# Mean aggregates of a graph network: gathered blocks stationary and one-hots of 64 columns moving, sums kept by feature

## The chip, the cores and the metric

One core of a Trainium2 chip runs the whole program. The metric is the device time of one execution in microseconds. TensorE (PE) multiplies; its weight loads are listed as PEld. VectorE is DVE, ScalarE is ACT, GpSimd is POOL and SyncE is SP. POOL issues the gathers, SP the plain loads and stores.

## What is computed

3125 nodes with 1024 features, 50000 edges sorted by destination. One attention layer (4 heads of 256) comes first, then two layers that take the mean over the incoming edges, all in float32. This change concerns the two mean layers:

```python
def _sage_layer(h, edge_src, edge_dst, deg_inv, W_self, W_neigh, b):
    msg = h[edge_src]
    agg = jax.ops.segment_sum(msg, edge_dst, num_segments=h.shape[0])
    mean = agg * deg_inv[:, None]
    return h @ W_self + mean @ W_neigh + b
...
h = jnp.maximum(_layernorm(x, axis=-1), 0.0)
x = x + _L0_gnn_ref(h, edge_index, ...)          # attention
h = jnp.maximum(_layernorm(x, axis=-1), 0.0)
deg_inv = 1.0 / jnp.maximum(deg, 1.0)
h1 = jax.nn.relu(_sage_layer(h, edge_src, edge_dst, deg_inv, W_self0, W_neigh0, b0))
x = x + _sage_layer(h1, edge_src, edge_dst, deg_inv, W_self1, W_neigh1, b1)
```

## The kernel before

Every float32 number is held as two float16 halves, high and low. A node's row is 2048 numbers of float16, 4096 bytes. A product of a tile with a 1024x1024 weight is 48 matmuls of 512 columns (high by high, high by low, low by high; 8 slices of the contraction, 2 halves of the columns), listed by `products`. Nodes stand in 25 tiles of 125 (TN). The program is a row of blocks, each of which begins when all engines have ended the one before: `prepare` (stage tab, tables and weight scales), the first norm and product (norm), edge scores, `weighted_sums` (gagg, the attention's sums), `gat_finish` (fin), `neighbours` (agg0, first mean, its product, relu), `sums_and_product` (agg1, second mean beside the product of the nodes' own rows), and `project` (neigh1, the product of the second mean).

A chunk is 128 edges in a row of the sorted list, cut so that it meets one tile; 415 chunks. In `prepare`, DVE places each chunk's tile and its edges (`place`, `own_row`), POOL fetches the edges' rows, PE turns the lists and DVE writes them as tables (`run_idx` the sources, `run_rel` the destinations within the tile, `run_tile` the tile). `place` runs its inner loop twice, once for the attention's order and once for that of the means.

In agg0 and agg1 POOL gathers the source rows of a chunk into one of R buffers (`got`; R is 9 and 8), 128 rows of 4 KB by an indirect DMA, as soon as PE has given the buffer back. DVE writes the one-hot mask of the chunk (`hot`, 128 edges x 128 destinations). PE holds the mask stationary and moves the gathered block, 4 matmuls of 512 columns (L2286 in agg0, L1839 in agg1). Chunks go in groups of two, or of one, 220 groups; DVE adds the sum of a group to the tile's row of `acc` (L2195, L1811), by nodes: 125 partitions x 1024 features. The group of a tile's end is followed by ACT (high half, times the inverse degree), DVE (low half, L2170), PE (16 turns of 128 columns), ACT (moves the turned halves), and 48 products in 6 pieces among the groups of the next tile (L2270), DVE's read with scale (L2178), ACT's relus (L2233), DVE's low half of the result (L2182), and SP's store. agg1 has the same ring, and the product of the nodes' own rows beside it (L1177). neigh1 takes the second mean from `acc`, splits it, turns it (L1072) and multiplies (L1090).

The order of each engine is that of the code; only semaphores connect them. On PE's queue the groups of a round and the pieces of the product stand in a fixed order.

Of the kernel before, what the change touches and what calls it, by code (L numbers as in the profile page):

```python
# [11 lines left out]
def bass_gat_sage_sage(nc, x_in, src_in, dst_in, w_gat, att_src, att_dst, gat_bias,  # L12
# [26 lines left out]
    RG = 8  # L39
    SB = 4  # L40
    CHUNKS = -(-E // CH) + NT - 1
    PAIRS = (CHUNKS - NT) // PAIR
    FOURS = (CHUNKS - 3 * NT) // 4
    GROUPS = PAIRS + NT
    EP = -(-(E + CH) // (CPP * CH))
    NCH = EP * CPP
    B = PAIR * RG
# [3 lines left out]
    paired = [min(PAIRS, CHUNKS * (r + 1) // (PAIR * NT)) for r in range(NT)]  # L51
    runs = [[tuple(range(PAIR * g, PAIR * (g + 1))) for g in range(paired[r - 1] if r > 0 else 0, paired[r])] + [(PAIR * PAIRS + r,)]
            for r in range(NT)]
# [23 lines left out]
    assert PAIR == 2 and PAIRS * PAIR + NT == CHUNKS and paired[-1] == PAIRS and NCH * CH >= E + CH and EP <= P and CHUNKS < NS  # L77
    assert 4 * FOURS + 3 * NT == CHUNKS and sum(len(cols) for cols in sets) == CHUNKS
    assert all(CHUNKS * (r + 1) // (PAIR * NT) <= PAIRS or CHUNKS * (r + 1) // NT - PAIR * PAIRS + NT - 1 - r <= r + 1 for r in range(NT))
# [101 lines left out]
    with top:  # L181
# [14 lines left out]
        run_idx = sb0("run_idx", [P, NS], i32)  # L196
        run_rel = sb0("run_rel", [P, NS])
        run_tile = sb0("run_tile", [1, NS], i32)
# [11 lines left out]
        deg_inv = sb0("deg_inv", [TN, NT])  # L210
        h1_up = sb0("h1_up", [P, 1])
        h1_down = sb0("h1_down", [P, 1])

        def tile_reg(engine, table, col):

            return nc.values_load_multi_w_load_instructions(
                table[0:1, col:col + 1], engines=[engine], min_val=0, max_val=NT - 1)[1][0]

# [5 lines left out]
        def prepare(key_r, mask_r, w16):  # L224
            with ExitStack() as ctx:
# [15 lines left out]
                start_c = sb("start_c", [P, NT - 1])  # L241
                first = sb("first", [P, NT + 1])
# [12 lines left out]
                run_size = sb("run_size", [P, 2, NT])  # L255
                run_begin = sb("run_begin", [P, 2, NT])
                run_shift = sb("run_shift", [P, 2, NT])
# [9 lines left out]
                pos_p = sb("pos_p", [SP_, 2, SB])  # L267
                own_p = sb("own_p", [SP_, 2, 2, SB])
                own_lo = sb("own_lo", [SP_, 2, SB])
                own_f = sb("own_f", [SP_, 2, SB])  # L270
                own_i = sb("own_i", [SP_, 2, SB], i32)
                own_got = sb("own_got", [SP_, 2, SB, 2 * CH], i32)
                own_rel = sb("own_rel", [SP_, 2, SB, CH])
# [1475 lines left out]
        def sums_and_product(tag, rows_in, acc, product):  # L1749

            with ExitStack() as ctx:
# [36 lines left out]
                def _(v):  # L1788
# [10 lines left out]
                    for k in range(1, R, 2):  # L1799
                        v.memset(got[:, k, :].bitcast(f32), 0.0).then_inc(blank[1], 1)  # L1800
                        if k // 2 < AHEAD:
                            make_hots(k // 2)
# [549 lines left out]
```

## Time and profile before

| what | us |
| --- | --- |
| runs of the kernel: median of 3 (lowest to highest) | 3293.75 (3290.86 to 3297.03) |
| profiled execution, first to last instruction (its span) | 3292.1 |
| of it: agg0 | 694 |
| of it: agg1 | 696 |
| of it: neigh1 | 296 |
| of it: tables (tab), about | 85 |
| PE busy / DVE busy / ACT busy / POOL busy | 2940.5 / 2208.3 / 1221.8 / 1517.3 |

The profiled execution lies 1.65 us under the median, within the spread of the runs. Stages follow one another, so a stage's share is read from a table of windows; what binds in a stage is read from the waits there, and not from the busy shares of the whole span. "Busy" of a matmul is a modelled end, so that the pace of a stream is better read from the starts of rows that follow each other.

### The profile page before, as it was taken

How to read it: one execution, taken by the hardware profiler on the slowest of the kernel's cores; microseconds unless marked ns; L12 is line 12 of the kernel's file. 1: busy time of each engine (PE TensorE's matmuls, PEld its weight loads, DVE VectorE, ACT ScalarE, POOL GpSimd, SP SyncE). 2: the span in 40 equal slices, each digit the busy share in tenths (PEclk: the TensorE clock that was granted, in tenths of full speed). 3: DMA queues.
4: the chain of work that ended last, by engine and by line, in shares of the span. 5: the costliest groups of instructions: out<-in, count | busy, mean ns of one | idle time of the engine just before them, and what ended most of it. 6: DMA issues, size and time to landing. Idle time of an engine off the chain costs nothing. (4 is left out here: it accounts for less than half of the span.)

```text
span 3292.1 us, 61715 instructions
## 1 busy us (share of the span) xinstructions
PE 2940.5 (89%) x19999; PEld 1682.0 (51%) x19999; DVE 2208.3 (67%) x3758; ACT 1221.8 (37%) x2818; POOL 1517.3 (46%) x1504
## 2 busy tenths in 40 slices
PE   5577998699999985999799999996899999998999
PEld 4344555388888873444244444443344444443444
DVE  8786878688888897888466666664455555555333
ACT  3564554598888883444122222222000000001111
POOL 2002232367777772222566666661565656552000
PEclk6688999899999998999899999998999999999999
DMA  2896996489999986776799999994999999996454
GB/s 80 273 294 212 330 311 204 157 303 363 348 361 349 352 300 202 219 219 210 293 338 350 343 353 350 363 360 165 358 340 321 340 333 339 324 355 233 137 142 126
DMA packets 271674, 934.22 MB, mean 284 GB/s; under 512 B 43263, under 2 KB 44267, under 8 KB 271375
## 3 DMA queue, kind: packets, MB, share of 16 engines
q0 software_dynamic: 206144, 709.74, 60.4%
q1 hardware_dynamic: 65230, 220.77, 21.4%
q8 instruction: 153, 2.51, 0.3%
q14 instruction: 147, 1.20, 0.1%
HBM read 838.14 MB, written 130.54 MB: 294 GB/s over the span
## 5 line engine op out<-in xcount | busy, mean ns | idle before, releaser
L1743 PE MATMUL gagg_sum_ps<-gagg_got,gagg_hot_hi 128*128 128x256 f16 x3320 | 575.8, 274 | 59.7 <-DVE sums_acc L1691 26.3
L1778 POOL DMA_INDIRECT agg_got<-h_rows,all_run_idx x415 | 412.6, 994 | 336.1 <-PE agg_sum_ps L1839 195.0
L1646 POOL DMA_INDIRECT gagg_got<-xs_rows,all_set_idx x415 | 460.3, 1109 | 169.4 <-issue 85.0
L1709 ACT ACTIVATE gagg_hot_hi<-gagg_hot,all_mem 128x128 f16<-128x128 f16 x1660 | 507.0, 387 | 81.3 <-DVE gagg_hot L1664 80.2
L2130 POOL DMA_INDIRECT agg_got<-h_rows,all_run_idx x415 | 420.8, 1014 | 251.1 <-PE agg_sum_ps L2286 139.7
L1811 DVE TENSOR_TENSOR sums_acc<-agg_sum_ps,sums_acc 125x1024 f32 x220 | 269.2, 1224 | 293.9 <-PE agg_sum_ps L1839 292.3
L1743 PE MATMUL gagg_sum_ps<-gagg_got,gagg_hot_lo 128*128 128x256 f16 x1660 | 454.8, 274 | 0.0
L1839 PE MATMUL agg_sum_ps<-agg_got,agg_hot 128*128 128x512 f16 x1660 | 400.3, 383 | 50.5 <-DMA agg_got<-h_rows,all_run_idx 40.4
L2195 DVE TENSOR_TENSOR sums_acc<-agg_sum_ps,sums_acc 125x1024 f32 x220 | 269.0, 1223 | 232.1 <-PE agg_sum_ps L2286 231.0
L2286 PE MATMUL agg_sum_ps<-agg_got,all_mem 128*128 128x512 f16 x1660 | 391.9, 382 | 22.4 <-DMA agg_got<-h_rows,all_run_idx 19.3
L1743 PEld LDWEIGHTS gagg_sum_ps<-gagg_got,gagg_hot_hi 128*128 128x128 f16 x3320 | 286.8, 97 | 111.3 <-DVE sums_acc L1691 38.0
L1839 PEld LDWEIGHTS agg_sum_ps<-agg_got,agg_hot 128*128 128x128 bf16 x1660 | 158.1, 98 | 257.5 <-DMA agg_got<-h_rows,all_run_idx 37.6
L2270 PE MATMUL agg_out_ps<-agg_w,all_mem 128*128 128x512 f16 x1200 | 283.8, 381 | 3.9 <-ACT all_mem L2225 3.9
L1177 PE MATMUL agg_out_ps<-agg_w,all_mem 128*128 128x512 f16 x1200 | 285.9, 381 | 0.0
L2286 PEld LDWEIGHTS agg_sum_ps<-agg_got,all_mem 128*128 128x128 bf16 x1660 | 160.8, 98 | 221.3 <-issue 27.3
L1669 DVE TENSOR_TENSOR gagg_hot_lo<-gagg_hot,all_mem 128x512 f16<-128x512 f16 x415 | 268.7, 687 | 3.6 <-DVE gagg_hot L1664 2.8
L1156 ACT ACTIVATE all_mem<-agg_turn_ps 128x2048 f16<-128x2048 f16 x25 | 46.9, 1877 | 598.7 <-PE agg_turn_ps L1164 598.7
L1090 PE MATMUL neigh_out_ps<-neigh_w,neigh_a_t 128*128 128x512 f16 x1176 | 259.3, 380 | 0.0
L1555 PE MATMUL edg_out_ps<-gatw_w,edg_a_t 128*128 128x512 f16 x1008 | 244.1, 387 | 16.3 <-ACT edg_rows L1363 16.3
L2270 PEld LDWEIGHTS agg_out_ps<-agg_w,all_mem 128*128 128x128 f16 x1200 | 117.8, 98 | 147.3 <-ACT all_mem L2225 4.3
L1177 PEld LDWEIGHTS agg_out_ps<-agg_w,all_mem 128*128 128x128 f16 x1200 | 118.1, 98 | 143.7 <-issue 3.6
L2217 ACT ACTIVATE all_mem<-sums_acc,all_deg_inv 125x1024 f16 x25 | 28.7, 1148 | 427.7 <-issue 392.7
(370 smaller groups left out, 4152.9 us busy)
## 6 DMA issues: line engine op xcount, KB each, us to landing
gatw_piece<-slot_rows POOLq DMA_DIRECT2D x52, 512.0 KB, 9.8
split_w<-edg_w_out SPq DMA_DIRECT2D x32, 512.0 KB, 7.7
agg_got<-h_rows,all_run_idx POOLq DMA_INDIRECT x830, 8.4
x_rows<-fin_val POOLq DMA_DIRECT2D x25, 500.0 KB
h_rows<-fin_h POOLq DMA_DIRECT2D x25, 500.0 KB
out_dram<-neigh_rows POOLq DMA_DIRECT2D x24, 500.0 KB, 3.6
norm_x_sb<-in_x_dram SPq DMA_DIRECT2D x25, 448.0 KB
fin_x_sb<-in_x_dram SPq DMA_DIRECT2D x25, 448.0 KB
```

The source lines that it names most:

```text
L1177: last = t.matmul(o, l, r, start=first, stop=final)
L1646: g.indirect_dma_start(out=got[:, u % R, :], out_offset=None, in_=rows_in[:, :], in_offset=bass.IndirectOffsetOnAxis(ap=set_idx[:, col:col ...
L1669: v.tensor_tensor(hot_lo[:, u % HOTS, :, :], hot[:, u % HOTS:u % HOTS + 1, :].to_broadcast([P, H, P]), weight_e[:, ds(begins[g] + j, 1), 1 ...
L1709: last = a.activation(hot_hi[:, u % HOTS, h, :], hot[:, u % HOTS, :], ACT.Copy, scale=high_e[:, ds(begins[g] + j, 1), h])
L1743: last = t.matmul(sum_ps[g % 2][:, h * C:(h + 1) * C], hot_k[:, u % HOTS, h, :], got[:, u % R, part * D + h * C:part * D + (h + 1) * C], s ...
L1778: g.indirect_dma_start(out=got[:, k % R, :], out_offset=None, in_=rows_in[:, :], in_offset=bass.IndirectOffsetOnAxis(ap=run_idx[:, col:col ...
L1811: v.tensor_tensor(acc[:, ds(tile, 1), 0:D], sum_ps[g % 2][0:TN, :].rearrange("p (a d) -> p a d", a=1), acc[:, ds(tile, 1), 0:D], ALU.add). ...
L1839: last = t.matmul(sum_ps[g % 2][:, q * HALF:(q + 1) * HALF], hot[:, u % R, :], got[:, u % R, over], start=(u == at[g] and part == 0), stop ...
L2130: g.indirect_dma_start(out=got[:, k % R, :], out_offset=None, in_=rows_in[:, :], in_offset=bass.IndirectOffsetOnAxis(ap=run_idx[:, col:col ...
L2195: v.tensor_tensor(acc[:, ds(tile, 1), 0:D], sum_ps[g % 2][0:TN, :].rearrange("p (a d) -> p a d", a=1), acc[:, ds(tile, 1), 0:D], ALU.add). ...
L2270: last = t.matmul(o, l, r, start=start, stop=stop)
L2286: last = t.matmul(sum_ps[g % 2][:, q * HALF:(q + 1) * HALF], hot[:, u % R, :], got[:, u % R, over], start=(u == at[g] and part == 0), stop ...
```

## The change

In both mean layers the gathered block of 128 edges becomes stationary, 16 slices of 128 features (8 high, 8 low), and the one-hot of the edges moves. The sum thus comes out by feature: 128 features on the partitions, the destinations along the columns. The one-hot has 64 columns. A tile of 125 destinations has two windows, of 64 and of 61; a chunk is visited once for the window it lies in, and the one chunk of a tile that holds the border is visited for both, which gives 415 + 25 = 440 visits. Each visit gathers, sums (16 matmuls of 64 columns, each with its own weight load) and adds 8 x 64 columns to the window of `flat`, whose place is read from a table (`win_at`) into a register for each visit. There are three sum buffers in PSUM, and masks are made four visits ahead. Since sums lie by feature, agg0 and neigh1 need no turns; ACT and DVE write the halves straight to `a_t`. The inverse degree goes from the halves to the read of the product (`post`, one column per tile), and the halves are scaled by a power of two from the largest degree. The products of agg0 are 12 pieces of 4 in the visits 2 to 13 of the next tile; agg1 has 15 pieces of 3 or 4 in a round of 17 visits. Turns of the nodes' own rows in agg1 stay. `prepare` counts the edges before each tile's border by 25 passes of ACT (`middles`), and places the visits (`place_windows`, `win_row`) in place of the second pass of the loop in `place`; POOL's second fetch waits for that.

```diff
-                        for k, (n, begins, sizes, shifts) in enumerate(((3, begin, size, shift), (2, run_begin, run_size, run_shift))):
...
+                    def place_windows():
...
+                        v.wait_ge(mid_summed, 1)
...
+                        inside_of(win_in[:, :, :], win_of[:, 0], step_w[:, :].unsqueeze(2).to_broadcast(natural), each(win_begin), each(visits))
...
+                        step(v.tensor_scalar(win_i[:, :], win_f[:, :], float(NCH - 1), None, ALU.min))
+                        v.sem_inc(win_ready, 1)
...
+                    g.wait_ge(win_ready, 1)
+                    for b in range(SB):
+                        g.indirect_dma_start(
+                            out=win_got[:, b, :], out_offset=None, in_=edge_rows[:, :],
...
+                            a.activation(junk_a[:, :, :], edges[:, :, 1, :], ACT.Sign, bias=mid_lines[:, t:t + 1],
+                                         accum_out=mid_signs[:, t:t + 1]).then_inc(mid_signed, 1)
...
+        def sum_window(t, u, sum_ps, got_u, hot_u):
+
+            for k in range(KT):
+                for part in range(2):
+                    last = t.matmul(sum_ps[:, k * WIN:(k + 1) * WIN], got_u[:, part * D + k * P:part * D + (k + 1) * P], hot_u,
+                                    start=(part == 0), stop=(part == 1))
+            return last
...
+        def by_feature(sums, tile):
+
+            return sums[:, ds(tile, 1), 0:D]
...
+        def window_of(flat, at):
+
+            return flat[:, ds(at, D)].rearrange("p (k d) -> p k d", k=KT)[:, :, 0:WIN]
```

The queues of agg0 (those of agg1 are alike, without `low`, `read` and `high`):

```diff
-                    for g, (i, n) in enumerate((i, n) for i, run in enumerate(runs) for n in range(len(run))):
-                        tile = tile_reg(mybir.EngineType.DVE, run_tile, seq[g][0])
-                        if g + AHEAD < GROUPS:
-                            make_hots(g + AHEAD)
-                        v.wait_ge(mm_done, at[g + 1] + R)
-                        v.wait_ge(added, g + 2)
-                        v.tensor_tensor(acc[:, ds(tile, 1), 0:D], sum_ps[g % 2][0:TN, :].rearrange("p (a d) -> p a d", a=1),
-                                        acc[:, ds(tile, 1), 0:D], ALU.add).then_inc(added, 1)
+                    for u, (i, n) in enumerate(place_of):
+                        at = at_reg(mybir.EngineType.DVE, u)
+                        if u + AHEAD < VISITS:
+                            make_hot(u + AHEAD)
+                        v.wait_ge(mm_done, u + 1)
+                        if u >= 1:
+                            v.wait_ge(added, u)
+                        v.tensor_tensor(window_of(flat, at), sum_ps[u % SUMS][:, :].rearrange("p (k d) -> p k d", k=KT), window_of(flat, at), ALU.add).then_inc(added, 1)
                         if n == LO_AT and i >= 1:
                             low(i - 1)
-                        if n == min(READ_AT, len(runs[i]) - 1) and i >= 2:
-                            read(i - 2)
+                        if n == READ_AT and i >= 1:
+                            read(i - 1)
...
-                            if n == TURN_AT and i >= 1:
-                                turn(i - 1)
...
-                                        last = t.matmul(sum_ps[g % 2][:, q * HALF:(q + 1) * HALF], hot[:, u % R, :], got[:, u % R, over],
-                                                    start=(u == at[g] and part == 0), stop=(u == at[g + 1] - 1 and part == 1))
...
-                    turn(NT - 1)
+                    for u, (i, n) in enumerate(place_of):
+                        t.wait_ge(arrived[u % R], 16 * (u // R + 1))
+                        t.wait_ge(hot_ready, u + 1)
+                        if u >= SUMS:
+                            t.wait_ge(added, u - SUMS + 1)
+                        sum_window(t, u, sum_ps[u % SUMS], got[:, u % R, :], hot[:, u % R, :]).then_inc(mm_done, 1)
...
+                        if MULTIPLY_AT <= n < MULTIPLY_AT + PIECES and i >= 1:
+                            multiply(i - 1, n - MULTIPLY_AT)
                     for piece in range(PIECES):
                         multiply(NT - 1, piece)
```

PE in the middle of agg0, before: the sums of a group (L2286), a piece of the product (L2270) and the turns of a tile (L2259).

```order
L2286 MATMUL agg_sum_ps<-agg_got,all_mem 128x512 x4
L2270 MATMUL agg_out_ps<-agg_w,all_mem 128x512 x8
L2286 MATMUL agg_sum_ps<-agg_got,all_mem 128x512 x16
L2259 MATMUL agg_turn_ps<-all_ident,all_mem 128x128 x16
L2286 MATMUL agg_sum_ps<-agg_got,all_mem 128x512 x16
```

After, in the same place: visits (L1833, 16 matmuls each) and pieces of 4 products (L2332).

```order
L2332 MATMUL agg_out_ps<-agg_w,all_mem 128x512 x4
L1833 MATMUL agg_sum_ps<-all_mem,agg_got 128x64 x16
L2332 MATMUL agg_out_ps<-agg_w,all_mem 128x512 x4
L1833 MATMUL agg_sum_ps<-all_mem,agg_got 128x64 x96
L2332 MATMUL agg_out_ps<-agg_w,all_mem 128x512 x4
```

The turns are gone, a piece is half as long, and six visits in a row stand without a product where a tile ends.

PE at the end of agg0, before: the last pieces, the last groups, and the products of the two last tiles.

```order
L2286 MATMUL agg_sum_ps<-agg_got,all_mem 128x512 x4
L2270 MATMUL agg_out_ps<-agg_w,all_mem 128x512 x32
L2286 MATMUL agg_sum_ps<-agg_got,all_mem 128x512 x4
L2259 MATMUL agg_turn_ps<-all_ident,all_mem 128x128 x16
L2270 MATMUL agg_out_ps<-agg_w,all_mem 128x512 x48
L2259 MATMUL agg_turn_ps<-all_ident,all_mem 128x128 x16
L2270 MATMUL agg_out_ps<-agg_w,all_mem 128x512 x48
```

After, at the same end:

```order
L1833 MATMUL agg_sum_ps<-all_mem,agg_got 128x64 x16
L2332 MATMUL agg_out_ps<-agg_w,all_mem 128x512 x4
L1833 MATMUL agg_sum_ps<-all_mem,agg_got 128x64 x64
L2332 MATMUL agg_out_ps<-agg_w,all_mem 128x512 x48
L2180 UNCONDITIONAL_BRANCH
```

Behind the last sums stands one tile's product, where there were two and the larger part of a third.

## Rows read from the trace of the kernel before

**Rows 1.** Table of windows, stages agg0, agg1, neigh1: window, length, busy, clock, share, GB/s

```profile
1596.00:2290.00 694.00, 654.34 (x3260) 300.08 (x3260) 437.93 (x704) 151.09 (x125) 415.48 (x412) 0.98 0.93 335
2300.00:2996.00 696.00, 656.15 (x3260) 299.58 (x3260) 383.14 (x659) 46.94 (x25) 410.20 (x414) 0.98 0.96 337
2996.00:3292.00 296.00, 284.62 (x1600) 141.51 (x1600) 110.87 (x104) 51.62 (x50) 12.61 (x24) 0.98 0.51 144
```

**Rows 2.** Waits in agg0 and agg1: who waits, for whom, us, times, longest

```profile
POOL agg_got L2130 <- PE agg_sum_ps L2286: 139.1, 144, 4.2
...
POOL agg_got L1778 <- PE agg_sum_ps L1839: 194.2, 162, 3.1
```

**Rows 3.** Table of windows, gathering stretches: PE, PEld, DVE, ACT, POOL, clock, DMA share, GB/s

```profile
1592.00:2240.00 648.00, 614.63 (x3067) 282.14 (x3068) 424.67 (x694) 135.72 (x113) 418.87 (x414) 0.98 0.99 356
2300.00:2990.00 690.00, 653.71 (x3251) 298.94 (x3252) 379.47 (x656) 46.94 (x25) 410.20 (x414) 0.98 0.97 340
```

**Rows 4.** DMA queues, 1600 to 2240, then 2300 to 2990: packets, MB, share (q0 gathers)

```profile
q0 software_dynamic: 59464, 203.74, 87.0%
q1 hardware_dynamic: 6867, 22.96, 11.2%
...
q0 software_dynamic: 59732, 204.75, 83.3%
q1 hardware_dynamic: 8611, 29.21, 13.6%
```

**Rows 5.** Table of windows, 2 us each in one tile of agg0

```profile
1936.00:1938.00 2.00, 2.00 (x11) 0.88 (x9) 2.00 (x6) 2.00 (x3) 1.67 (x2) 1.00 0.81 266
1942.00:1944.00 2.00, 2.00 (x11) 0.90 (x10) 2.00 (x4) 0.00 (x0) 1.53 (x2) 1.00 1.06 264
1952.00:1954.00 2.00, 2.00 (x11) 0.88 (x9) 1.34 (x3) 0.00 (x0) 1.48 (x2) 1.00 1.03 408
```

**Rows 6.** Timeline of POOL, agg0's last gather: start, us, engine, idle before and why

```profile
2235.75 1.00 POOL L2130 DMA_INDIRECT agg_got<-h_rows,all_run_idx  x1 [0.30 <-issue]
```

**Rows 7.** Timeline of PE in the norm stage: three sorts of matmul in a row

```profile
244.48 1.06 PE L915 MATMUL norm_turn_ps<-all_ident,norm_a 128*128 128x128 f16 x16
245.37 0.75 PE L924 MATMUL norm_att_ps<-gatw_w_att,norm_a_t 128*128 128x8 f16 x24
245.98 0.81 PE L938 MATMUL norm_out_ps<-gatw_w,norm_a_t 128*128 128x512 f16 x3
```

**Rows 8.** Groups by line on DVE: count, busy us, mean ns, idle before

```profile
L2195 DVE TENSOR_TENSOR sums_acc<-agg_sum_ps,sums_acc 125x1024 f32 x220 | 269.0, 1223 | 232.1 <-PE agg_sum_ps L2286 231.0
...
L1049 DVE SCALAR_TENSOR_TENSOR neigh_rows<-neigh_out_ps,neigh_post,neigh_rows 125x512 f32<-125x512 f32 x2 | 1.5, 752 | 6.3 <-PE neigh_out_ps L1090 3.6 <-PE neigh_out_ps L1084 2.7
```

**Rows 9.** Timeline of agg0's end and the next stage's first instruction

```profile
2259.94 12.93 PE L2270 MATMUL agg_out_ps<-agg_w,all_mem 128*128 128x512 f16 x48 [1.97 <-ACT all_mem L2225]
...
2286.30 1.28 DVE L2178 SCALAR_TENSOR_TENSOR all_mem<-agg_out_ps,agg_post,all_mem 125x1024 f32<-125x1024 f32 x1 [7.30 <-PE agg_out_ps L2270]
...
2295.41 3.89 ACT L1820 ACTIVATE agg_got<-all_ones 128x1024 f32<-128x1024 f32 x4 [5.60 <-PEq L120]
```

**Rows 10.** Chain that ended last, in neigh1: start, us, what; the last two repeat

```profile
3006.39 11.68 PE neigh_out_ps L1090 x48
3018.07 0.89 PE neigh_turn_ps L1072 x16
3018.97 10.36 PE neigh_out_ps L1090 x48
```

**Rows 11.** Timeline of DVE in the tables' stage

```profile
55.17 0.37 DVE L490 TENSOR_TENSOR tab_within<-tab_pos_p,tab_run_begin 104x200 f32<-104x200 f32 x1
...
66.00 4.87 DVE L601 SCALAR_TENSOR_TENSOR gatw_w<-tab_w_sb,all_w_up,gatw_w 128x1024 f16<-128x1024 f32 x4
```

**Rows 12.** Table of windows, end of agg1

```profile
2976.00:2980.00 4.00, 2.27 (x9) 0.75 (x10) 2.89 (x6) 0.00 (x0) 3.09 (x4) 1.00 1.03 415
...
2992.00:2997.00 5.00, 0.90 (x4) 0.19 (x2) 2.43 (x2) 0.00 (x0) 0.00 (x0) 0.83 0.00 0
```

More of the change, by code:

```diff
@@ L674, in _ @@
                     weigh(KT - 1)
+                    t.wait_ge(mid_counted, 1)
+                    t.matmul(mid_ps, ones[0:EP, :], mid_below[:, :], start=True, stop=True).then_inc(mid_summed, 1)
                     t.wait_ge(own_tiles, 1)
@@ L1175, in multiply @@
                     t.wait_ge(read_out, i + 1)
-                for o, l, r, first, final in todo[piece * per:(piece + 1) * per]:
+                for o, l, r, first, final in todo[piece * len(todo) // pieces:(piece + 1) * len(todo) // pieces]:
                     last = t.matmul(o, l, r, start=first, stop=final)
@@ L1763, in sums_and_product @@
                 blank = [sem(f"blank{i}") for i in range(2)]
-                seq = [cols for run in runs for cols in run]
-                at = [sum(len(cols) for cols in seq[:g]) for g in range(len(seq) + 1)]
-                assert at[-1] == CHUNKS and len(seq) == GROUPS >= RG * (NT + 1)
+                assert BEGIN + ROUND * NT <= VISITS and 2 + PIECES == ROUND
                 block = ctx.enter_context(nc.Block())
@@ L2019, in _ @@
                             bound()
+                            sum_scale()
                         if m >= 2:
@@ L2079, in _, with neighbours @@
                         last.then_inc(prod_done, 1)
-        def neighbours(tag, rows_in, wi, add, rows_out, acc, mem):
+        def neighbours(tag, rows_in, wi, add, rows_out, flat, sums, mem):
             with ExitStack() as ctx:
@@ L2086, in neighbours @@
                 R = 9
[L2087 to L2093 removed]
+                SUMS = 3
+                AHEAD = 4
+                LO_AT, MULTIPLY_AT, READ_AT, OUT_AT = 0, 2, 14, 16
+                PIECES = 12
                 carve = carver(mem)
@@ L2204, in _ @@
+                    v.wait_ge(added, VISITS)
                     low(NT - 1)
-                    for j in (NT - 2, NT - 1):
-                        read(j)
-                        out_low(j)
+                    read(NT - 1)
+                    out_low(NT - 1)
                 @block.scalar
                 def _(a):
-                    def high(j):
+                    for k in range(0, R, 2):
+                        a.activation(got[:, k, :].bitcast(f32), ones[:, 0:1].to_broadcast([P, D]), ACT.Copy, scale=0.0).then_inc(blank[0], 1)
@@ L2212, in high @@
+                    for j in range(NT):
                         tile = tile_reg_at(mybir.EngineType.Activation, j)
[L2213 to L2218 removed]
@@ L2228, in relu @@
+                        a.wait_ge(lo_done, j + 1)
+                        a.activation(sums[:, ds(tile, 1), 0:D], ones[:, 0:1].to_broadcast([P, D]).rearrange("p (a d) -> p a d", a=1),
+                                     ACT.Copy, scale=0.0).then_inc(zeroed, 1)
                         a.wait_ge(read_out, j + 1)
```

570 lines of the change are left out of this document (288 added, 282 removed).

## The prediction

> **What bounds the kernel now.** I read the table of stages first. Of the 3292.1 us of the span the change touches mainly three stretches: the first aggregate (agg0), the second (agg1) and the last product (neigh1), 694, 696 and 296 us [rows 1]. In agg0 and agg1 TensorE is busy 94% and the DMA share reads 0.93 and 0.96, so the table alone does not tell which of the two sets the pace. The waits do: the queue of GpSimd, which issues the gathers, stands 139.1 us in agg0 and 194.2 us in agg1 until TensorE has given a gather buffer back [rows 2]. In the stretches in which gathers run, TensorE is busy 614.63 of 648 and 653.71 of 690 us [rows 3]. Counted in columns this agrees: at 10.36 us for 48 products of 512 columns [rows 10], 0.216 us each, one aggregate has 1660 sums (358 us), 1200 products (259 us) and 25 turns of 0.89 us (22 us), 639 us. So TensorE holds the ring. Right behind it stand the transfers: their share is 0.99 and 0.97, but at only 356 and 340 GB/s [rows 3], whereas short stretches with the ring full carry 408 to 415 [rows 5, 12]. In neigh1 the chain of waits is TensorE alone, 48 products, 16 turns, 48 products and so on [rows 10].
>
> **TensorE in agg0 and agg1.** Each visit is 16 pairs of a 128x128 weight load and a 64-column matmul. No row shows that width. Its neighbours: 24 pairs with 8 columns go from 245.37 to 245.98, 25.4 ns a pair; 16 pairs with 128 columns from 244.48 to 245.37, 55.6 ns [rows 7]. Both are at full clock with a new stationary block each time, so loads hide behind their neighbours. By columns 64 should lie at half of 55.6 and a little more; I take 29.5, ends 25.4 and 55.6. A visit is then 0.47 us (0.41 to 0.89), 440 visits 208 us instead of 358. With 259 us of products agg0 needs 467 us (438 to 650) and agg1, which keeps its turns, 489 (460 to 672), where 639 stood: TensorE no longer sets the pace unless the pair costs what the 128-column one does. The Trainium skill ("TensorE: Matmul & The Clock Gate", section "Back-to-back issue gap") speaks against this: it gives about 81 ns for each pair of weight load and 128-column matmul in a stream. By it a visit is 1.30 us and each aggregate over 820 us; the trace disagrees, with 55.6 ns for just such pairs.
>
> **What is late next.** Three candidates stand close together.
> GpSimd: one gather every 1.295 us when nothing holds it (1.00 busy, 0.30 issue) [rows 6]; 440 instead of 415 make 570 us, under 648 and 690.
> VectorE: a visit adds 512 elements per lane instead of 1024 for a pair (1.22 us [rows 8]; half of the width with the fixed part kept is near 0.70, as 0.75 for 512 elements out of PSUM shows [rows 8]), writes one mask of 64 columns where a pair wrote two of 128, and loads a register that the shorter add hides no longer fully. I take 1.0 us, bounds 0.9 and, if nothing shrinks with width, 1.5. With 3.8 us of a tile's own steps (three passes like the 1.28 of [rows 9]) agg0 needs 17.6 x 1.0 + 3.8 = 21.4 us a tile, agg1 about 19, against 25.9 and 27.6 a tile now.
> The transfers: the bytes are unchanged, since rows outside a window are skipped as the ones outside a tile were. In the 640 us window of agg0 the gathers take 87.0% of the engines' time for 203.74 MB, the direct transfers 11.2% for 22.96 MB [rows 4]: 2.73 and 3.12 us per MB. With the ring full a share of 1.03 moves 0.411 MB per us [rows 5, 12], 2.51 us per MB. If all gathers went so, 203.74 x 2.51 + 71.7 = 583 us of share, over 1.03 566 us, in 648 us 573: a gain of 75 at most. In agg1 likewise 204.75 x 2.51 + 93.8 = 607, over 1.03 589, a gain of 101 at most. At least it is 0. Two slow kinds of moments stand in a tile's round: one while GpSimd has just been let go and fills an emptied ring (266 GB/s at a share of 0.81), one while the direct loads and stores of the tile run (264 GB/s at 1.06) [rows 5]. The first goes with TensorE's hold on the ring, the second stays. I take half of each bound: **agg0 -38, agg1 -50** (bounds 0 to -75 and 0 to -101). A tile of agg0 then takes 24.4 us, above GpSimd's 22.8, VectorE's 21.4 and TensorE's 18.7.
>
> **The end of agg0.** Now the last gather is issued at 2235.75 [rows 6], and the stage after starts at 2295.41 [rows 9]. Between lie two tiles' products that were put off, two sets of 48 (the first 12.93 us, begun at half clock) with their turns, and the last tile's read, two relus, the low half and the store; from 2286.30, where the products end, to 2295.41 these take 9.1 us [rows 9]. From landing at about 2240 that is 55 us. After, products of a tile run inside the next tile's visits, so one tile is left: last sum 0.5, add 0.7, high and low half 2.5 (two passes like the 1.28 of the read [rows 9]), one set 12.9 at the same clock, and 9.1: about 26, with the handovers 27. **-28** (-20 to -32). In agg1 the last pieces and the last store end beside the last visits, as now: +2 (-2 to +6).
>
> **neigh1.** 25 turns go. 23 of them are 0.89 us each (3018.97 less 3018.07), 20.5 us; the first product begins at 3006.39 [rows 10], 10 us after the stage's start at 2996, and needs then only two short scale steps and the high and low halves, 3.5 with the handovers: -6.5. The turns also warmed the clock; without them I add 2 us of products at half clock. **-25** (-20 to -28). By-feature reads on ScalarE and VectorE lie beside 10.36 us of products.
>
> **Tables and small things.** VectorE is the chain of the first stage. It loses a second pass of its place loop and gains some 20 small steps for the windows; at about a third of a microsecond a step, as the 0.37 of [rows 11], 11 steps or 3.5 us against 6.6; the second fetch is issued only after them, and its four issues, 5.2 us [rows 6], with some 2 of landing lie beside 4.87 us of low halves [rows 11], so some 3 show, and handovers add 2 to the 3 of steps. The 25 added passes on ScalarE are spread between its copies, and I take them to end before the windows are placed. **+8** (+4 to +12; if ScalarE becomes the chain, +20). Largest degree in the attention stages: +1.5.
>
> **The sum**, on the profiled execution: 3292.1 - 38 - 28 - 50 + 2 - 25 + 8 + 1.5 = 3160.6. That execution's span is 1.65 us under the median of the runs shown, 3293.75, so the median should be 3162. Own range of this course: 0 to -75 and 0 to -101 for the phases, the other bounds beside it: 3085 to 3255.
>
> **Rivals.**
> *The gathers gain nothing* (share 0.99 and 0.97 already means full): then only -28 + 2 - 25 + 8 + 1.5 = -41.5 is left, 3252. For it: the shares [rows 3]. Against: 408 to 415 GB/s where the ring is full [rows 5, 12]. The Trainium skill ("SBUF - State Buffer", section "Summary: rules for kernel authors") would have it so, with about 358 GB/s for transfers between memory and SBUF; agg0's mean of 356 looks like it, but 408 to 415 GB/s over several microseconds disagree. Chance 0.17.
> *Weight loads do not hide* (slower): the trace shows a LDWEIGHTS beside every matmul, and where one must be waited for, the pair may reach 55.6 ns and more. With what the stretches hold beside TensorE's 639 us (9 and 51 us) it sets both paces again from about 52.5 ns; above that both together cost 14.1 us per ns, and the 41.5 us won elsewhere are used up at 55.5 ns, all but the price of the 128-column pair. At 81 ns the two would take 829 and 851 us and the kernel some 3600. Against: both rows of [rows 7]. Chance 0.07.
> *VectorE becomes the bound* (slower when far): from 1.17 us a visit in agg0 it takes over from the transfers, and from 1.42 in both (880 visits and 127 us of other steps against 1338 plus 41.5) nothing is won; at 1.5 us the two take 755 and 690, the kernel about 3360. For: a register load and four instructions per visit in a row, one add that waits for the one before. Chance 0.07.
> *The clock falls*: products sit in 12 of 17.6 visits of agg0; in the other five or six TensorE is busy about a third of the time. With TensorE busy 2.27 of 4 us the clock read full, 2.4 GHz, and with 0.90 of 5 us it read 0.83, a part of it at 1.2 GHz [rows 12]. If half of each round ran at 1.2 GHz, a tile would need 18.7 x 1.5 = 28 us: agg0 at 700 instead of 610, 3252. Against: the ring holds nine blocks and the products that follow raise it again. Chance 0.06.
>
> **How the numbers follow.** The forecast's course has 0.63, the gathers' rival 0.17, weights 0.07, VectorE 0.07, clock 0.06. Forecast time 3162. The range takes the forecast's bounds and the first rival: 3085 to 3260; left out are weights, VectorE's far end, and a little below. A measurement of this kernel can tell about 0.2% (6.6 us) from no change. Slower by more: weights 0.06, VectorE 0.05, clock 0.01 and 0.01 for tables that cost far more than bounded: 0.13. Within: 0.04. Faster: 0.83.
>
> **What would show it.** Right: in the profile after, TensorE's busy share in both aggregates near 75%, the wait of GpSimd for TensorE smaller or gone, GB/s near 375 in agg0 and 365 in agg1, a visit of 16 matmuls in about 0.47 us, 27 us from the last landing to agg1's start, neigh1 near 271 us with nothing between sets of 48 products, the first stage 8 us longer. Wrong: LDWEIGHTS and matmuls of a visit that take 0.9 us or more; VectorE busy over 95% with TensorE waiting for its adds; a granted clock of 0.5 in parts of each round; or GB/s as before while everything else idles.

## The result, and the profile after

The changed kernel takes 3245.95 us (median of 4 runs, 3237.43 to 3248.66) beside 3292.48 us of the kernel before: a ratio of 0.985, 95% interval 0.9835 to 0.9866. It is faster by 46 us where 130 were forecast. The time lies in the stated range, the gain at a third of the forecast.

Where the time went is read from the gathers, whose first and last issues cut the span of 3247.0 us into five stretches.

| stretch | before | after | forecast | measured |
| --- | --- | --- | --- | --- |
| start to agg0's first gather | 1589.8 | 1607.5 | +9.5 | +17.7 |
| agg0, first to last gather | 646.0 | 676.6 | -38 | **+30.6** |
| to agg1's first gather | 61.5 | 40.2 | -28 | -21.3 |
| agg1, first to last gather | 687.1 | 643.1 | -50 | -44.0 |
| to the end | 307.6 | 279.5 | -23 | -28.1 |

One term has the wrong sign and holds 69 of the 85 us that are missing: agg0's gathering. How well a stretch repeats is read from the other profiles: agg1 with this code took 638 to 657 us in seven of them, agg0 with the same code within 3 us of itself.

Tables of windows of the kernel after, to set beside [rows 1, 3]: agg0's gathers, agg1's gathers, neigh1; columns as there.

```profile
1607.00:2284.00 677.00, 531.86 (x8028) 355.28 (x8029) 474.20 (x940) 105.70 (x98) 468.39 (x439) 0.84 0.96 344
2324.00:2967.00 643.00, 524.85 (x8534) 347.80 (x8534) 427.29 (x899) 49.27 (x28) 434.24 (x439) 0.95 1.01 364
2976.00:3247.00 271.00, 260.72 (x1200) 117.53 (x1200) 93.60 (x79) 28.59 (x25) 12.62 (x24) 0.99 0.55 158
```

agg0 moves 344 GB/s where it moved 356, with TensorE busy only 79% of the time and a mean clock of 0.84. agg1 rose from 340 to 364. neigh1 takes 271 us, as forecast.

The waits of agg0 after, to set beside [rows 2]:

```profile
POOL agg_got L2224 <- PE agg_sum_ps L1833: 90.3, 85, 2.7
...
PE agg_sum_ps L1833 <- DVE sums_acc L2288: 64.6, 49, 2.0
PE agg_out_ps L2332 <- issue: 54.8, 23, 3.2
PE agg_sum_ps L1833 <- DMA agg_got<-h_rows,all_win_idx: 28.0, 15, 15.3
```

GpSimd still waits for TensorE, now 90.3 us. TensorE is hardly waiting for gathers (28.0 us, all of it before the first product at 1647.5): it waits for VectorE's adds (64.6 us), which stand in VectorE's queue behind the read of the product, and once in each of 23 tiles ahead of a piece of the product (54.8 us). That last wait is in front of the first piece. One tile's round shows why. Timeline of agg0 after, one round, rows of PE, DVE and ACT:

```profile
1900.76 0.63 PE L1833 MATMUL agg_sum_ps<-all_mem,agg_got 128*128 128x64 f16 x16
...
1901.22 1.03 PE L2332 MATMUL agg_out_ps<-agg_w,all_mem 128*128 128x512 f16 x4
...
1902.09 0.63 PE L1833 MATMUL agg_sum_ps<-all_mem,agg_got 128*128 128x64 f16 x16
...
1908.73 2.23 PE L1833 MATMUL agg_sum_ps<-all_mem,agg_got 128*128 128x64 f16 x64
...
1910.33 1.28 DVE L2270 SCALAR_TENSOR_TENSOR all_mem<-agg_out_ps,agg_post,all_mem 125x1024 f32<-125x1024 f32 x1
...
1911.65 2.19 ACT L2318 ACTIVATE all_mem<-all_mem,all_h_up 125x1024 f32<-125x1024 f32 x2 [19.49 <-DVE all_mem L2270]
...
1913.74 1.13 ACT L2309 ACTIVATE all_mem<-sums_acc,all_sum_up 128x1024 f16 x1
1913.87 1.23 DVE L2274 TENSOR_TENSOR all_mem<-all_mem 125x1024 f16<-125x1024 f32 x1 [0.60 <-ACT all_mem L2318]
...
1915.78 1.28 DVE L2263 SCALAR_TENSOR_TENSOR all_mem<-sums_acc,all_sum_up,all_mem 128x1024 f16<-128x1024 f16 x1
...
1917.15 1.87 PE L2332 MATMUL agg_out_ps<-agg_w,all_mem 128*128 128x512 f16 x4 [3.11 <-issue]
...
1918.81 1.06 PE L1833 MATMUL agg_sum_ps<-all_mem,agg_got 128*128 128x64 f16 x16
...
1919.68 1.89 PE L2332 MATMUL agg_out_ps<-agg_w,all_mem 128*128 128x512 f16 x4
```

First, the sum itself is as cheap as forecast: 1901.22 less 1900.76 is 0.46 us for 16 pairs, 28.8 ns a pair. Second, a visit with a piece goes from 1900.76 to 1902.09, 1.33 us, above GpSimd's 1.295 [rows 6], so in the twelve of them TensorE holds the ring. Third, when the last piece ends at 1908.73, a chain runs over three engines before the next first piece: read (L2270), relus and then the high half on ACT (L2318, L2309), low half of the result and of the sums on DVE (L2274, L2263). It takes 8.4 us here; worked out from the starts of all pieces it is 9.9 us in the median of 23 rounds (8.4 to 11.1). In it TensorE finds six sums, 2.8 us of work, and stops at the first piece, whose place in its queue bars it from the sums behind. Fourth, the pieces after the chain run at half clock: 1919.68 less 1918.81 is 0.87 us for the same 16 pairs. The median product phase, first piece to last, is 17.8 us, where it is 15.5 at full clock (e1_warm, below). These medians add to 27.7; the mean tile, 676.6 / 25, is 27.1 us.

The clock along this round, table of windows:

```profile
1900.00:1908.00 8.00, 8.00 (x123) 5.15 (x120) 5.51 (x12) 0.00 (x0) 5.96 (x7) 1.00 0.95 344
1908.00:1917.00 9.00, 4.18 (x102) 3.34 (x98) 7.63 (x13) 3.23 (x3) 7.10 (x7) 0.94 0.91 311
1917.00:1923.00 6.00, 5.85 (x43) 3.23 (x44) 3.31 (x9) 1.06 (x1) 2.89 (x3) 0.52 1.02 328
```

TensorE is busy 8.00 of 8, then 4.18 of 9 us, and starts the next pieces at a clock of 0.52, mostly 1.2 GHz.

### The profile page after: what moved, and what is told of

It reads as the page before. It is cut to its first block and busy times, and to the rows that moved or that the text cites. A ratio compares the mean times of both kernels' runs of the same rounds, so it can differ in the third digit from the quotient of the medians.

```text
span 3247.0 us, 84374 instructions
## 1 busy us (share of the span) xinstructions
PE 2693.6 (83%) x29961; PEld 1778.2 (55%) x29961; DVE 2289.9 (71%) x4237; ACT 1176.4 (36%) x2818; POOL 1593.5 (49%) x1558
## 5 line engine op out<-in xcount | busy, mean ns | idle before, releaser
L2224 POOL DMA_INDIRECT agg_got<-h_rows,all_win_idx x440 | 469.4, 1067 | 233.2 <-issue 117.3
L1868 POOL DMA_INDIRECT agg_got<-h_rows,all_win_idx x440 | 435.4, 990 | 247.9 <-PE agg_sum_ps L1833 123.1
L1899 DVE TENSOR_TENSOR sums_acc<-agg_sum_ps,sums_acc 128x512 f32 x440 | 304.4, 692 | 173.9 <-PE agg_sum_ps L1833 170.2
L2288 DVE TENSOR_TENSOR sums_acc<-agg_sum_ps,sums_acc 128x512 f32 x440 | 304.1, 691 | 165.2 <-PE agg_sum_ps L1833 159.0
L2332 PE MATMUL agg_out_ps<-agg_w,all_mem 128*128 128x512 f16 x1200 | 349.0, 420 | 63.4 <-issue 54.8
L1833 PEld LDWEIGHTS agg_sum_ps<-all_mem,agg_got 128*128 128x128 f16 x7040 | 280.0, 103 | 188.9 <-issue 98.0
L1833 PEld LDWEIGHTS agg_sum_ps<-agg_hot,agg_got 128*128 128x128 f16 x7040 | 259.0, 100 | 219.7 <-DMA agg_got<-h_rows,all_win_idx 160.7
L1833 PE MATMUL agg_sum_ps<-all_mem,agg_got 128*128 128x64 f16 x7040 | 297.6, 201 | 96.2 <-DVE sums_acc L2288 64.6
L1833 PE MATMUL agg_sum_ps<-agg_hot,agg_got 128*128 128x64 f16 x7040 | 283.2, 197 | 104.1 <-DMA agg_got<-h_rows,all_win_idx 103.0
L1256 PE MATMUL agg_out_ps<-agg_w,all_mem 128*128 128x512 f16 x1200 | 330.6, 389 | 26.6 <-DVE all_mem L1230 26.6
L2318 ACT ACTIVATE all_mem<-all_mem,all_h_up 125x1024 f32<-125x1024 f32 (+1 forms) x50 | 54.7, 1141 | 485.4 <-DVE all_mem L2270 485.4
L1159 PEld LDWEIGHTS neigh_out_ps<-neigh_w,neigh_a_t 128*128 128x128 f16 x1176 | 115.2, 98 | 146.7 <-issue 8.6
L2332 PEld LDWEIGHTS agg_out_ps<-agg_w,all_mem 128*128 128x128 f16 x1200 | 105.1, 104 | 157.5 <-issue 97.5
```

The costliest lines, as they stand in the source:

```text
L1159: last = t.matmul(o, l, r, start=start, stop=stop)
L1256: last = t.matmul(o, l, r, start=first, stop=final)
L1833: last = t.matmul(sum_ps[:, k * WIN:(k + 1) * WIN], got_u[:, part * D + k * P:part * D + (k + 1) * P], hot_u, start=(part == 0), stop=(par ...
L1868: g.indirect_dma_start(out=got[:, u % R, :], out_offset=None, in_=rows_in[:, :], in_offset=bass.IndirectOffsetOnAxis(ap=win_idx[:, u:u + 1 ...
L1899: v.tensor_tensor(window_of(flat, at), sum_ps[u % SUMS][:, :].rearrange("p (k d) -> p k d", k=KT), window_of(flat, at), ALU.add).then_inc( ...
L2224: g.indirect_dma_start(out=got[:, u % R, :], out_offset=None, in_=rows_in[:, :], in_offset=bass.IndirectOffsetOnAxis(ap=win_idx[:, u:u + 1 ...
```

## The experiments

Theory A: agg0's round is a loop through TensorE's queue, made of bunched pieces, a chain between tiles, and a cold clock. Theory B: agg0 waits for its transfers, whose share reads 0.96. Times by stage are windows from the first to the last gather. Ratios are to the kernel before, run beside each.

**Work in the idle stretch** (e1_warm):

```diff
                         if MULTIPLY_AT <= n < MULTIPLY_AT + PIECES and i >= 1:
                             multiply(i - 1, n - MULTIPLY_AT)
+                        elif i >= 1:
+                            for q in range(4):
+                                t.matmul(junk_ps[:, :], w16[:, q, 0:P], w16[:, q, 0:HALF], start=True, stop=True)
```

> The changed kernel, and in agg0 four more matmuls of 512 columns in each visit that has no piece of the product; their sums go to an unused bank and are read by nobody. Theory A (a tile's round on TensorE is a loop: twelve product visits of 1.33 us, then a chain of 8.4 us from the last piece through read, relu, high and low half to the next first piece, after which the first pieces run at half clock): the added work fills the chain's idle time, the granted clock stays at 1.0 and the 2.7 us a tile lost at half clock come back: agg0 from 677 to about 610 to 630 us, the kernel 3180 to 3200. Theory B (agg0 waits for its transfers, share 0.96): no change or slower, 3245 to 3270.

```profile
1600.00:2228.00 628.00, 575.60 (x8591) 373.00 (x8592) 475.15 (x944) 105.30 (x98) 464.81 (x439) 0.97 1.00 371
```

3205.65 us, ratio 0.9719 (0.9681 to 0.9758). More work on TensorE made agg0 49 us shorter, at 0.97 of the clock and 371 GB/s. The half clock is thus worth about 2 us a tile; the chain stays as long as it was (9.9 us), the product phase falls to 15.5, and the two add to 25.4 beside a mean tile of 25.1. Theory B falls: the same bytes came 8% faster. The kernel lies 6 us above the expected range; agg1, which this edit leaves alone, took 657 us in the profile.

**The chain shortened by order alone** (e4_order):

```diff
-                        if n == OUT_AT and i >= 1:
-                            out_low(i - 1)
+                        if n == 1 and i >= 2:
+                            out_low(i - 2)
...
+                        a.activation(as_turned(a_t, 0), by_feature(sums, tile), ACT.Copy, scale=sum_up[:, 0:1]).then_inc(hi_done, 1)
+                        if j >= 1:
+                            relu(j - 1)
+                        a.wait_ge(lo_done, j + 1)
```

> The changed kernel, and in agg0 the chain between two tiles' products made shorter by order alone: ScalarE takes the high half of a tile before the relus of the tile before, and VectorE's low half of the result moves from visit 16 to visit 1 of the tile after, behind the low half of the sums. Theory A: the first piece starts about 1.2 us sooner in each of 24 rounds, agg0 -20 to -45 us, the kernel 3200 to 3225. Theory B: 3240 to 3250.

```profile
1603.00:2233.00 630.00, 514.36 (x8048) 343.58 (x8048) 472.12 (x941) 101.06 (x98) 457.29 (x439) 0.89 1.00 368
```

3195.75 us, 0.9708 (0.9677 to 0.9738). agg0 lost 46 us, one more than the expected range allows, and the kernel lies 4 us below its range: the median chain went from 9.9 to 8.2 us where 1.2 less was expected. The product phase hardly changed (17.5), and the mean clock went from 0.84 to 0.89: some rounds now start their pieces at full clock (four products in 1.02 us at 1918.05), others still at half (1.87 at 1941.67).

**The product spread over the round** (e5_spread):

```diff
-                LO_AT, MULTIPLY_AT, READ_AT, OUT_AT = 0, 2, 14, 16
-                PIECES = 12
+                LO_AT, MULTIPLY_AT, READ_AT, OUT_AT = 0, 2, 18, 20
+                PIECES = 16
...
-                a_t = carve([P, 2, KT, P], f16)
+                a_ts = [carve([P, 2, KT, P], f16) for _ in range(2)]
...
+                        if j >= 1:
+                            relu(j - 1)
+                    relu(NT - 1)
```

The relus also move behind the next tile's high half, as in e4_order, so that this edit shortens the chain too.

> The changed kernel, and in agg0 the product spread over the round: 16 pieces of 3 in visits 2 to 17 after a tile's end instead of 12 pieces of 4 in visits 2 to 13, with two buffers for the turned halves, and the read and the result's low half two and four visits later than the round's end. Theory A: a product visit costs 0.47 + 0.65 = 1.12 us, below GpSimd's 1.30, no chain stands between two tiles, the clock stays at 1.0; agg0 goes to 600 to 640 us (as agg1's 643), the kernel 3170 to 3210. Theory B: agg0 stays above 660, the kernel above 3230.

```profile
1614.00:2235.00 621.00, 505.60 (x8038) 328.30 (x8039) 475.05 (x939) 106.02 (x97) 463.10 (x439) 0.92 1.01 373
2274.00:2924.00 650.00, 533.29 (x8534) 351.73 (x8534) 429.04 (x900) 49.17 (x28) 434.25 (x439) 0.93 1.00 360
```

```profile
PE agg_sum_ps L1833 <- DMA agg_got<-h_rows,all_win_idx: 73.8, 73, 15.8
PE agg_out_ps L2341 <- DVE all_mem L2274: 43.8, 23, 3.0
```

3193.43 us, 0.9688 (0.9665 to 0.971). agg0 takes 621 us, 25 under the kernel before, and TensorE now waits for gathers (73.8 us). Two parts of the expectation did not come: 43.8 us of waiting for the read are left ahead of the first pieces, and the clock reads 0.92 instead of 1.0.

**What is left without TensorE** (e2_few_products):

```diff
-                        for o, l, r, start, stop in todo[piece * per:(piece + 1) * per]:
+                        for o, l, r, start, stop in {0: todo[0:2], PIECES - 1: todo[-2:]}.get(piece, []):
```

> The changed kernel with 44 of the 48 products of each tile left out in agg0 (the first two and the last two stay), so that its output is not the reference's; gathers, sums, adds, and the rest of a tile's steps stay. Theory A: TensorE no longer holds the ring, and agg0 falls from 677 to GpSimd's or the transfers' pace, 575 to 615 us; the kernel 3165 to 3200. Theory B (the transfers bind agg0 now): agg0 stays within 20 us of 677.

```profile
1612.00:2226.00 614.00, 382.81 (x7022) 320.01 (x7022) 474.20 (x942) 105.47 (x98) 463.19 (x439) 0.71 1.02 378
```

3181.26 us, and agg0 614: at a clock of 0.71, with hardly any products, agg0 is only 7 us under e5_spread. So that is nearly what the rest of the stage needs, and a cold clock costs nothing where TensorE has time.

**What sets those 614 us** (e6_spread_half), half of each row left out in both aggregates:

```diff
-                            out=got[:, u % R, :], out_offset=None, in_=rows_in[:, :],
+                            out=got[:, u % R, 0:D], out_offset=None, in_=rows_in.rearrange("n (a d) -> (n a) d", a=2),
```

> The kernel of e5_spread with half of each gathered row left out in agg0 and agg1 (2 KB instead of 4, so that its output is not the reference's); as many gathers, and all matmuls, adds and stores as there. Theory C (with TensorE out of the way the transfers set the pace of both aggregates): agg0 from 621 and agg1 from 650 both fall to GpSimd's bare issue pace, 440 times 1.295 = 570, to 570 to 585 us. Theory D (GpSimd's issuing, with the gathers that take longer than 1 us, or VectorE holds them): agg0 stays at 610 to 621, agg1 at 630 to 650.

```profile
1605.00:2202.00 597.00, 500.45 (x8102) 332.56 (x8103) 477.95 (x946) 106.03 (x97) 463.29 (x440) 0.92 0.74 220
2236.00:2817.00 581.00, 508.13 (x8568) 350.48 (x8569) 428.70 (x901) 49.20 (x28) 439.19 (x439) 0.96 0.78 229
```

GpSimd's waits in agg0, and its gathers in agg0 and agg1 (count | busy, mean ns of one):

```profile
POOL agg_got L2228 <- issue: 100.2, 329, 0.3
POOL agg_got L2228 <- PE agg_sum_ps L1833: 32.9, 108, 0.3
...
L2228 POOL DMA_INDIRECT agg_got<-h_rows,all_win_idx x440 | 464.1, 1055 | 158.9 <-issue 100.2
L1868 POOL DMA_INDIRECT agg_got<-h_rows,all_win_idx x440 | 440.2, 1000 | 175.3 <-issue 93.5
```

3100.41 us. With 43% fewer bytes (581 us at 229 GB/s for 650 at 360) agg1 falls by 69 us, to 581, nearly GpSimd's 570: there theory C holds, the transfers set the pace. agg0 falls by 24, to 597, between the two theories. What keeps the other 27 us over 570 is GpSimd itself: it stands for no buffer longer than 0.3 us, but a gather takes 1.055 us in the mean, since 34 of the 440 take 1.11 to 2.06 us, 24 us more than 0.99 each. All but one of the 34 lie beside VectorE's passes for a low half (L2267, L2278); agg1 has no such pass and no gather over 1.05 us.

**Two product buffers, and the tables** (e7_tables, e8_best). In e7_tables the windows are placed ahead of the first fetch's rows (TensorE's sum for them moves ahead too), in e8_best this is joined to e5_spread with a second bank for the product, the last two lines.

```diff
-                    place()
                     v.wait_ge(mid_signed, NT)
                     v.tensor_scalar(mid_below[:, :], mid_signs[:, :], -0.5, 0.5 * CPP * CH, ALU.mult, ALU.add).then_inc(mid_counted, 1)
+                    place()
...
+                    place_windows()
                     own_row()
-                    place_windows()
...
-                out_ps = ps("out_ps", [P, D])
+                out_pss = [ps(f"out_ps{b}", [P, D]) for b in range(2)]
```

> The changed kernel, and in the tables' stage the count at the borders summed ahead of the last weighing and the windows placed ahead of the first fetch's rows, so that the second fetch is issued some 7 us earlier. Theory A (VectorE's chain there holds 3.6 us of waiting for the first fetch and 4.2 us for the second, both because the windows are placed late): the norm's first work moves from 95.3 to 87 to 90 us, the kernel 5 to 8 us less than 3246. Rival (the added passes of ScalarE or the added steps of VectorE are the whole price): 94 to 95.5 us, no change.

> The kernel of e5_spread with two buffers for the product's sum in agg0, so that a tile's first piece no longer waits for the read of the tile before (43.8 us of waits in e5_spread), and with the tables of e7_tables. Theory A, by which TensorE is off the path already in e5_spread: agg0 615 to 622, only the tables' 5 to 8 us are gained, the kernel 3182 to 3192. Rival (these waits still hold the ring): agg0 below 605, the kernel below 3175.

e7_tables: 3248.58 us, 0.9858 (0.9831 to 0.9885), no difference from the changed kernel that can be told. The norm's first work moved from 95.3 to 92.4 us, 2.9 of the 5 to 8 expected. Its timeline of GpSimd says why:

```profile
64.98 1.47 POOL L434 DMA_INDIRECT tab_win_got<-edge_rows,tab_win_i  x1 [4.83 <-DVEq L649]
66.76 1.01 POOL L434 DMA_INDIRECT tab_win_got<-edge_rows,tab_win_i  x1 [0.30 <-issue]
68.07 5.54 POOL L434 DMA_INDIRECT tab_win_got<-edge_rows,tab_win_i  x1 [0.30 <-issue]
73.91 1.01 POOL L434 DMA_INDIRECT tab_win_got<-edge_rows,tab_win_i  x1 [0.30 <-issue]
```

The fetch is issued 5.8 us sooner, but one of its four gathers takes 5.54 us instead of 1.01, just while VectorE runs its four passes over the weights (67.86 to 72.7). The next three kernels, with the same tables, have one of 5.54 us too. e8_best: 3188.84 us, 0.9694 (0.9646 to 0.9741), agg0 618 us, not told apart from e5_spread; TensorE was off the path already.

**The ring** (e9_best_ring, e10_ring10, e12_before_ring9): nine buffers instead of eight in agg1, then ten in both, and nine in agg1 of the kernel before.

```diff
-                R = 8
+                R = 9
```

> The kernel of e8_best with nine gather buffers in agg1 instead of eight. If the ring's length is what keeps agg1 (643 to 650) above agg0 (621 with nine): agg1 falls to 620 to 635, the kernel 10 to 25 us under e8_best. If its own direct transfers do: agg1 within 8 us of e8_best's.

> The kernel of e9_best_ring with ten gather buffers in both aggregates (there nine and nine). If the ring is still what keeps the aggregates above what GpSimd's pace of 570 us allows: agg0 from 621 to 605 to 614, agg1 from 624 to 608 to 616, the kernel 3140 to 3158. If nine are enough and the transfers' own rate is the limit: both within 6 us of 621 and 624, the kernel 3160 to 3170.

> The kernel before with nine gather buffers instead of eight in its second aggregate, nothing else. If TensorE set the pace there, as the prediction read it (639 us of columns in 690): agg1 from 687 to 675 to 687. If the ring's length did: agg1 below 670, the kernel below 3275.

Windows of agg1 in e9_best_ring, of agg0 and agg1 in e10_ring10, of agg1 in e12_before_ring9:

```profile
2261.00:2885.00 624.00, 521.16 (x8532) 346.98 (x8533) 426.33 (x898) 49.94 (x29) 435.55 (x440) 0.95 1.02 375
```

```profile
1602.00:2211.00 609.00, 490.20 (x8018) 314.12 (x8019) 472.46 (x934) 105.75 (x97) 458.69 (x439) 0.96 1.02 379
2252.00:2874.00 622.00, 519.13 (x8512) 344.41 (x8513) 426.57 (x897) 50.31 (x29) 434.60 (x440) 0.96 1.02 376
```

```profile
2299.00:2963.00 664.00, 644.02 (x3234) 299.62 (x3235) 378.00 (x654) 50.03 (x29) 412.90 (x415) 0.98 0.99 352
```

TensorE's waits for gathers in agg1, in the kernel before and in e12_before_ring9:

```profile
PE agg_sum_ps L1839 <- DMA agg_got<-h_rows,all_run_idx: 40.4, 26, 20.0
...
PE agg_sum_ps L1839 <- DMA agg_got<-h_rows,all_run_idx: 24.3, 8, 20.0
```

e9_best_ring: 3167.85 us, 0.9622 (0.9605 to 0.9638); agg1 from 649 to 624 by one buffer. e10_ring10: 3163.07 us, 0.9608 (0.9586 to 0.963), the lowest median of the kernels that leave nothing out; agg0 gained 11 us, as its first theory had it, agg1 2, as its second, so a ring of nine was enough in agg1. e12_before_ring9: 3274.38 us, 0.9948 (0.9925 to 0.9972); agg1 fell from 687 to 664. This went against the reading that TensorE alone set the pace there before: with eight buffers it waited 40.4 us for gathers, with nine 24.3 (20.0 of each at the stage's start). That its bunched pieces (8 products in a row) are what eight buffers could not ride over is likely, and not tested.

**The weights' passes moved away from the fetch** (e11_pass_later):

```diff
-                    for k in range(KT // 2):
-                        low(k)
                     win_row()
...
-                    for k in range(KT // 2, KT):
+                    for k in range(KT):
                         low(k)
```

> The kernel of e9_best_ring with the four passes of VectorE over the weights (L695, 4.9 us in a row) taken from beside the second fetch of the tables' stage and put behind it. If these passes hold GpSimd's gathers (one of 5.54 us in e7_tables, 2.02 and 2.09 in the changed kernel, against 0.99 elsewhere): the four gathers take 1.0 to 1.2 us each and the fetch is issued in 5.3 us; the stage ends within 1.5 us of before, since the passes come later. If something else lengthens them: one of them still takes over 1.5 us, and the stage ends 3 to 5 us later.

```profile
64.53 1.47 POOL L434 DMA_INDIRECT tab_win_got<-edge_rows,tab_win_i  x1 [4.84 <-DVEq L649]
66.30 1.01 POOL L434 DMA_INDIRECT tab_win_got<-edge_rows,tab_win_i  x1 [0.30 <-issue]
67.61 1.01 POOL L434 DMA_INDIRECT tab_win_got<-edge_rows,tab_win_i  x1 [0.30 <-issue]
68.93 1.01 POOL L434 DMA_INDIRECT tab_win_got<-edge_rows,tab_win_i  x1 [0.30 <-issue]
```

The last three gathers take 1.01 us, so the passes held the one of 5.54; the first keeps the 1.47 us that it had in e7_tables, outside the expected 1.0 to 1.2. The stage ends only 1 us sooner (92.1 for 93.2), since the passes come later; the kernel at 3165.53 us is not told apart from e9_best_ring.

## Why the prediction was wrong

**TensorE's price: right.** 28.8 ns a pair against 29.5 taken, 0.46 us a visit. The rival in which weights do not hide is out. The rule of "Back-to-back issue gap" (the Trainium skill, "TensorE: Matmul & The Clock Gate"), 81 ns for a pair with 128 columns, does not hold in these traces, which have 55.6 [rows 7].

**agg0's gathering: wrong, and the step is the comparison of averages.** The prediction set a tile's totals side by side, transfers 24.4, GpSimd 22.8, VectorE 21.4, TensorE 18.7 us, and took the largest. TensorE's 18.7 us were placed, not spread. The code shown in the change put twelve pieces into visits 2 to 13, each of 1.33 us, over GpSimd's 1.295 by its own prices (0.47 + 0.86); it gave the product one buffer of halves and one sum, so that a first piece must wait for the read, the high and the low half; and the order fence showed six visits in a row without a piece. The text named the six visits only in the clock's rival, and never asked who is queued behind the first piece. What came instead is a round of 27.1 us for the 24.4 forecast, a loop of product phase and chain. e1_warm takes away its half clock alone and brings 49 us of the 69, e4_order mainly shortens the chain and brings 46, e5_spread spreads the pieces, shortens the chain and adds a buffer at once and brings 55. The three overlap and are not shares that add up. With the loop off the path the term is 646 to 621, -25 (e5_spread), or -28 (e8_best), within its bounds and short of the -38.

**GpSimd's pace: too low.** The 22.8 us a tile took each gather at 1.00 us. Gathers of the changed kernel, agg0 and agg1:

```profile
L2224 POOL DMA_INDIRECT agg_got<-h_rows,all_win_idx x440 | 469.4, 1067 | 233.2 <-issue 117.3
L1868 POOL DMA_INDIRECT agg_got<-h_rows,all_win_idx x440 | 435.4, 990 | 247.9 <-PE agg_sum_ps L1833 123.1
```

In agg0 one takes 1.067 us in the mean, 1.014 before the change: 43 of 440 take 1.13 to 2.04 us, all but the first beside a low-half pass of VectorE (L2263, L2274), where 19 of 415 took over 1.1 us before. With 0.30 between them that is 24.1 us a tile, as late as the 24.4 of the transfers. It did not hold agg0 in the changed kernel, but e6_spread_half shows that it does once TensorE and the transfers are out of the way.

**The clock's rival** came closer than its 0.06: it named the place and a tile of 28 us, 3252 us; 27.1 and 3246 were measured, its sign, a clock near 0.5 in a part of each round, came (0.52), and filling the idle stretch alone gives back about 2.0 of the 2.7 us by which the tile exceeds the forecast (e1_warm). Its size is partly luck: it put half of each round at half clock, where some 5 us of the round shown are (1917 to 1922), and it had no chain. I gave it 0.06 because the ring would carry over it. A ring carries over a stretch in which TensorE is late only if TensorE is faster than the gathers afterwards, and at 1.33 us a visit it was not.

**agg1: right** in size (-44 for -50, known to some 10 us by the spread of its profiles). The mechanism was only half read: e12_before_ring9 gets 24 us there from one more buffer without the change.

**The rival in which gathers gain nothing** is out: with whole rows the share read 0.96 to 1.02 in both aggregates, while the rate went from 340 to 379 GB/s. The rule of about 358 GB/s (the Trainium skill, "SBUF - State Buffer", section "Summary: rules for kernel authors") is passed by a whole stage of 609 us at 379 GB/s in e10_ring10.

**The end of agg0: -21 for -28.** Timeline of the stage's end after, POOL's last gather, the last product and its read, to set beside [rows 9]:

```profile
2284.15 0.99 POOL L2224 DMA_INDIRECT agg_got<-h_rows,all_win_idx  x1 [0.34 <-issue]
...
2300.48 12.77 PE L2332 MATMUL agg_out_ps<-agg_w,all_mem 128*128 128x512 f16 x48 [7.54 <-DVE all_mem L2263]
2313.39 1.28 DVE L2270 SCALAR_TENSOR_TENSOR all_mem<-agg_out_ps,agg_post,all_mem 125x1024 f32<-125x1024 f32 x1 [13.02 <-PE agg_out_ps L2332]
```

The last product begins 16.3 us after the last issue, where the forecast had about 8 (4 to the landing, 0.5, 0.7 and 2.5): the pieces of the tile before and the chain still stand in front of it.

**neigh1 and agg1's end: -28 for -23.** From the last gather to neigh1's start it is -2 where +2 was taken, neigh1 itself -26 for -25. The chain of waits after, in neigh1, to set beside [rows 10]; start, us, what:

```profile
2981.55 10.57 DMA neigh_w<-split_w
2992.17 239.75 PE neigh_out_ps L1159 x1110
```

Without turns 1110 products follow one another with no other work between. The first product now waits for the load of the weights, which the turns used to cover, 1.1 us longer than for its low half. The prediction added 2 us because the turns had warmed the clock. They had not: it read 0.50 in the turns and 0.65 as the products began (3006.4 to 3010), and the first set of 48 took 11.68 us where later ones take 10.36 [rows 10]. So 1.3 us were lost there before, and 1.6 after (11.99).

**Tables: +9.4 for +8**; ScalarE's passes end before the windows are placed, as taken. Of the 17.7 us up to agg0's first gather 8.3 are left, for the 1.5 of the largest degree. Where they come from is open: from the norm's first work to that gather eleven profiles with the change took 1505 to 1519 us, the two without it 1504, and the products of the edge scores alone, which no kernel here alters, 341 to 355.

**The sums.** The terms add to -129.5, so that the span's 3160.6 should have read 3162.6. With both gathering terms at their far bounds the sum gives 3076 on the runs, not 3085. And at 81 ns the 3600 leaves out the 9 and 51 us held beside TensorE's work; by its own terms it is some 3650. None of this decides anything.

## What to carry to other kernels

When a change frees an engine, do not compare totals per round: walk its queue once through the round and price each place where it must wait in order, the dearest visit against the pace of what feeds it, and the chain from the last use of a single buffer to its next. Price the issuing engine too with what runs beside it, and not by one undisturbed gather. Work spread more evenly (here 3 products a visit instead of 4, with a second buffer and a shorter chain) took TensorE off the path, although its clock still read 0.92. A busy share near 1 on the transfers did not mean that they were the bound (0.96 at 344 GB/s, 1.01 at 373 for the same gathers).

## What the hardware showed

VectorE's passes over the weights (L695, float16 from float32) hold GpSimd's gathers: 5.54 us for one beside four such passes, 2.02 and 2.09 in the changed kernel, 1.01 with the passes elsewhere. The passes for a low half in agg0 go with the same: 43 gathers of the changed kernel take 1.13 to 2.04 us there, where 0.99 is usual, 42 of them beside such a pass, and none of agg1's, which has no such pass, is over 1.04. No run here moved those. The Trainium skill ("SBUF - State Buffer", section "Summary: rules for kernel authors") says that descriptors made by GpSimd starve while VectorE runs in its 2x or 4x modes. No trace here names the mode; the lengthened gathers agree with it.

TensorE held 28.8 ns for a pair of a 128x128 weight load and a matmul of 64 columns at 2.4 GHz, and 54 ns (0.87 us for 16) at 1.2 GHz.
